# Attention over positions: block keys and values fetched by SyncE, queries read in place, score products of 64 x 64

## The reference

```python
x = x + attn(cond(x, cond_1024))         # causal attention inside each sequence, one head
h = cond2(x, cond_1024)                  # x + x @ layer, a matrix of its own for each sequence
# "ffn" on h, with S = 32 sequences as the attended axis and 256 positions as the batch:
ln1 = layer_norm(h); qkv = ln1 @ qkv_weight.T          # 16 query heads, 4 key/value heads, head size 16
scores = q . k * 16 ** -0.5, causal over the 32 sequences; attn = softmax(scores)
h1 = h + (attn @ v) @ proj_weight.T
# mixture of 8 experts, two per token: router, gelu(x @ w1) @ w2, weighted sum
x = x + h1 + moe(layer_norm(h1))
```

## Time and profile before

| | |
|---|---|
| time, median of 3 runs | 1201.92 us (1200.04 to 1207.69) |
| span of the profiled execution | 1207.2 us |
| time of the profiled execution | 1207.69 us (the only one of the three that is not shorter than the span) |
| opening | 0 to 399 us |
| positions' loop (mask products L1333) | 399.2 to 711.0 us |
| experts, overlapping the loop's end | from about 720 us to the end |
| busy over the span | PE 1128.8 (94%), PEld 1016.7 (84%), DVE 910.1 (75%), ACT 824.1 (68%), POOL 587.6 (49%) |
| mean granted TensorE clock | 0.968 of full speed |

### The profile page before, as it was taken

How to read it: one execution, slowest core, us unless ns; L and a number is a source line. 1 busy time by engine, 2 the same in 40 slices (tenths; PEclk the granted TensorE clock), 3 DMA queues, 4 the chain that set the end, 5 groups by cost and what they waited for, 6 DMA issues and landing times. The chain is left out here.

```text
span 1207.2 us, 25130 instructions
## 1 busy us (share of the span) xinstructions
PE 1128.8 (94%) x8180; PEld 1016.7 (84%) x8180; DVE 910.1 (75%) x2230; ACT 824.1 (68%) x1869; POOL 587.6 (49%) x564
## 2 busy tenths in 40 slices
PE   7899999999999899998998998899999999999994
PEld 4699999999998688877787776789998899889884
DVE  5677777677775579888898886897877777777872
ACT  2466666766666588887886778557677766776671
POOL 0012212122222144787888786678865454555446
PEclk9899999999999899998999998989999999999998
DMA  9533435343331022344444355578887686777654
GB/s 300 125 106 122 121 114 161 109 140 118 99 104 54 18 80 80 116 133 134 129 133 135 111 170 180 161 174 218 196 198 180 167 194 179 188 182 175 166 141 63
DMA packets 117838, 171.25 MB, mean 142 GB/s; under 512 B 13584, under 2 KB 88752, under 8 KB 117680
## 3 DMA queue, kind: packets, MB, share of 16 engines
q1 hardware_dynamic: 91120, 135.43, 36.7%
q0 software_dynamic: 26592, 34.24, 14.9%
HBM read 103.76 MB, written 67.69 MB: 142 GB/s over the span
## 5 line engine op out<-in xcount | busy, mean ns | idle before, releaser
L1311 POOL DMA_INDIRECT out_rows<-y,row x142 | 235.4, 1658 | 173.1 <-DVE y L1931 129.6
L1862 DVE TENSOR_TENSOR hl<-h,hh 128x512 fp32r<-128x512 f32 (+1 forms) x156 | 99.7, 642 | 83.7 <-ACT h L1530 73.0
L178 PE MATMUL gh<-w2h,hh 128*128 128x256 f32 x568 | 159.7, 281 | 1.1 <-issue 1.1
L180 PE MATMUL gh<-w2h,hl 128*128 128x256 f32 x568 | 159.8, 281 | 0.0
L179 PE MATMUL gh<-w2l,hh 128*128 128x256 f32 x568 | 159.6, 281 | 0.0
L1529 ACT ACTIVATE hh<-gw 128x512 fp32r<-128x512 f32 (+1 forms) x78 | 44.1, 565 | 126.9 <-issue 125.2
L1289 POOL DMA_INDIRECT slot_rows<-kept,slot x104 | 112.0, 1077 | 29.6 <-issue 28.4
L178 PEld LDWEIGHTS gh<-w2h,hh 128*128 128x128 f32 x568 | 107.8, 190 | 2.3 <-issue 1.2
L844 POOL TENSOR_SCALAR spread<-mv 128x2 f32<-128x2 f32 x32 | 7.0, 218 | 210.1 <-DVE mv L992 209.8
L179 PEld LDWEIGHTS gh<-w2l,hh 128*128 128x128 f32 x568 | 107.9, 190 | 1.1
L180 PEld LDWEIGHTS gh<-w2h,hl 128*128 128x128 f32 x568 | 107.8, 190 | 0.0
(11 more groups left out here) (338 smaller groups left out, 3945.9 us busy)
## 6 DMA issues: line engine op xcount, KB each, us to landing
w1e<-in_moe_w SPq DMA_DIRECT2D x39, 512.0 KB
w2e<-in_moe_w SPq DMA_DIRECT2D x39, 512.0 KB
xr<-slot_rows SPq DMA_DIRECT2D x32, 532.0 KB
x_rows<-x SPq DMA_DIRECT2D x64, 256.0 KB, 2.5
xg<-x_rows SPq DMA_DIRECT2D x62, 256.0 KB
xT<-in_xT SPq DMA_DIRECT2D x32, 256.0 KB, 2.8
x<-in_x SPq DMA_DIRECT2D x32, 256.0 KB, 3.7
out_rows<-res SPq DMA_DIRECT2D x64, 128.0 KB
```

What stands on the lines that cost most here:

```text
L178: nc.tensor.matmul(out, at_a(ah), at_b(bh), start=first, stop=False, skip_group_check=True)
L180: return nc.tensor.matmul(out, at_a(al), at_b(bh), start=False, stop=last, skip_group_check=True)
L1311: g.indirect_dma_start(out=out, out_offset=bass.IndirectOffsetOnAxis(ap=row[m % NR][:, t:t + 1], axis=0), in_=y[m % 2][:, t, :], in_offset ...
L1862: v.tensor_tensor(hl[m % 2][:, f, 0:n], h[:, f, 0:n], hh[m % 2][:, f, 0:n].bitcast(F32), ALU.subtract).then_inc(hl_did, 1)
```

## The change

Keys and values are no longer spread by VectorE. Three SBUF tensors, `keys0`, `keys1` and `values`, each for both places, are zeroed by GpSimd once; for every step SyncE copies the keys of each head into its block of columns, twice (once for each partition half), by 8 transfers, and the values by 8 more, from SBUF to SBUF. Keys have two buffers, values one. The queries are read where they are (`pr.heads`), with positions ahead of the channel half in their layout, so ScalarE's copies and VectorE's multiplication are gone. The scores of a place and position are two products of 64 rows x 64 columns x 128, one per partition half; TensorE does one half of both places, the transposes of place 0's values, the other half of both places, and the transposes of place 1's. The value product's output goes to both partition halves of `ps_w` in two products of 64 moving columns, and ScalarE takes it with one copy of 128 partitions. In the opening, `xT` and `stack` now share memory with `keys0` and `values`, and SyncE issues step 0's transfers at its end. SyncE's hardware loop is written out, each load stands ahead of its store, and the transfers of steps 1 and 2 go ahead of the loop, those of step j + 3 at the start of its step j.

```diff
@@ Program
+        self.keys0 = sb("keys0", [P, U2, NKV, TG, S])
+        self.values = sb("values", [P, U2, TG, NKV, S])
...
+    def fetch_keys(self, sp, keys, k):
+        groups = slice(U2 * k, U2 * (k + 1))
+        for side in range(2):
+            for g in range(NKV):
+                sp.dma_start(keys[side * NKV * HD + g * HD:side * NKV * HD + (g + 1) * HD, :, g].rearrange("p u t s -> p u (t s)"),
+                             self.kv[g * HD:(g + 1) * HD, groups].rearrange("p g t s -> p g (t s)")
+                             ).then_inc(self.keys_in[k % 2], 16)
+
+    def fetch_values(self, sp, k):
+        for g in range(NKV):
+            rows = slice((NKV + g) * HD, (NKV + g + 1) * HD)
+            for u in range(U2):
+                sp.dma_start(self.values[rows, u, :, g], self.kv[rows, U2 * k + u]).then_inc(self.values_in, 16)
@@ opening, SyncE
             pipeline(step, 0, I1 + 2)
+            sp.wait_ge(pr.cleared, 2)
+            for u in places:
+                after(sp, dve_did["kv"], I1 - 1, u)
+            pr.fetch_keys(sp, pr.keys0, 0)
+            pr.fetch_values(sp, 0)
@@ opening, GpSimd
-            pipeline(step, -2, I1 + 2)
+            pipeline(step, -2, I1 + 1)
+            for u in places:
+                after(pool, dve_did["u"], I1 - 1, u)
+            g.memset(pr.keys0[:], 0.0).then_inc(pr.cleared, 1)
+            for u in places:
+                after(pool, pe_did["layer"], I1 - 1, u)
+            g.memset(pr.values[:], 0.0).then_inc(pr.cleared, 1)
+            pipeline(step, I1 + 1, I1 + 2)
@@ rows_and_experts, SyncE
+            def blocks(k):
+                if k == 1:
+                    sp.wait_ge(pr.cleared, 3)
+                else:
+                    after(sp, pe_did["score"], k - 2, U2 - 1)
+                pr.fetch_keys(sp, keys[k % 2], k)
+                after(sp, pe_did["vT"], k - 1, U2 - 1)
+                pr.fetch_values(sp, k)
+
             def step(j):
+                if j + 3 < I2:
+                    blocks(j + 3)
+                if j == EARLY_STORES:
+                    sp.wait_ge(pr.planned, 1)
+                    sp.wait_ge(pr.scattered[0], 16 * K * EARLY_GROUPS)
                 for u in places:
                     after(sp, pool_did["res"], j, u)
                     if j + 1 < LAST:
                         load(j + 1, u)
                     store(j, u)
+            for u in places:
+                load(0, u)
+            for k in (1, 2):
+                blocks(k)
+            for j in range(EARLY_STORES):
+                step(j)
@@ TensorE
+            def score(k, u, side, t):
+                rows = slice(side * KV1, (side + 1) * KV1)
+                return t_.matmul(ps_s[u][rows, t * P:(t + 1) * P], pr.heads[rows, group(k, u), t, :],
+                                 keys[k % 2][rows, u, :, t, :], start=False, stop=True, skip_group_check=True)
...
                         t_.matmul(ps_s[u][:], pr.identb[:], pr.causalb[:].rearrange("p t g s -> p (t g s)"),
                                   start=True, stop=False, skip_group_check=True)
-                        after(pe, act_did["q"], k, u)
-                        after(pe, dve_did["kv"], k, u)
-                        for t in range(TG):
-                            ins = t_.matmul(ps_s[u][:, t * P:(t + 1) * P], qg[u][:, t].rearrange("p j s -> p (j s)"),
...
-                        ins.then_inc(pe_did["score"], 1)
+                    pe.wait_ge(pr.keys_in[k % 2], 16 * 2 * NKV * (k // 2 + 1))
+                    for t in range(TG):
+                        for u in places:
+                            score(k, u, u, t)
+                    pe.wait_ge(pr.values_in, 16 * U2 * NKV * (k + 1))
+                    values(k, 0)
+                    for t in range(TG):
+                        for u in places:
+                            ins = score(k, u, 1 - u, t)
+                            if t == TG - 1:
+                                ins.then_inc(pe_did["score"], 1)
+                    values(k, 1)
...
-                            ins = t_.matmul(ps_w[u][0:KV1, t * P:(t + 1) * P], vb[(k - 1) % 2][u][:, t, :],
-                                            pwT[u][:, t].rearrange("p j s -> p (j s)"), start=True, stop=True)
+                            for side in range(2):
+                                rows = slice(side * KV1, (side + 1) * KV1)
+                                ins = t_.matmul(ps_w[u][rows, t * KV1:(t + 1) * KV1], vb[(k - 1) % 2][u][:, t, :],
+                                                pwT[u][:, t, 2 * side:2 * side + 2].rearrange("p j s -> p (j s)"),
+                                                start=True, stop=True)
@@ ScalarE
-                if has(k + 1):
-                    heads(k + 1, 0)
...
-                        for jp in range(2):
-                            ins = a.copy(aoT[u][jp * KV1:(jp + 1) * KV1], pairs[:, jp])
-                        ins.then_inc(act_did["ao"], 1)
+                        a.copy(aoT[u][:], ps_w[u][:, 0:TG * KV1].rearrange("p (t h s) -> p h t s", t=TG, h=2)
+                               ).then_inc(act_did["ao"], 1)
@@ VectorE
-                if has(k + 1):
-                    for u in places:
-                        heads(k + 1, u)
-                        next(route, None)
@@ program
-            pr.q = kept[:, :, 0:DC * P].rearrange("p g (c t s) -> p c g t s", c=DC, t=TG)
+            pr.q = kept[:, :, 0:DC * P].rearrange("p g (t c s) -> p c g t s", c=DC, t=TG)
+            pr.heads = kept[:, :, 0:DC * P].rearrange("p g (t n) -> p g t n", t=TG)
```

More of the change, by code:

```diff
@@ L382, in __init__ @@
         self.blank = sb("blank", [P, ROW])
+        self.keys_in = [self.sem(f"keys_in{n}") for n in range(2)]
+        self.values_in, self.cleared = self.sem("values_in"), self.sem("cleared")
         self.scattered = [self.sem(f"scattered{k}") for k in range(3)]
@@ L431, in opening @@
         x = bufs("x", [P, TC, D])
-        xT = bufs("xT", [P, DC, T])
-        stack = bufs("stack", [STACK, 2, D])
+        xT = [pr.keys0[:, u].rearrange("p g t s -> p (g t s)").rearrange("p (c n) -> p c n", c=DC) for u in places]
+        stack = [pr.values[0:STACK, u].rearrange("p t g s -> p (t g s)").rearrange("p (k n) -> p k n", k=2) for u in places]
         uT = parts("uT", [P, DC, T])
@@ L1054, in rows_and_experts @@
         KV1 = NKV * HD
-        qg = brief("qg", [KV1, TG, JQ, S])
-        kvd = brief("kvd", [P, TG, NKV, S])
-        last12 = [a[:].rearrange("p t g s -> p (t g s)").rearrange("p (k n) -> p k n", k=2) for a in kvd]
+        keys1 = passing.enter_context(nc.sbuf_tensor("keys1", [P, U2, NKV, TG, S], F32))
+        keys = [pr.keys0, keys1]
+        last12 = [pr.keys0[:, u].rearrange("p g t s -> p (g t s)").rearrange("p (k n) -> p k n", k=2) for u in range(U2)]
         rows12 = lambda j, u: last12[u] if j == LAST else x12[u][:]
@@ L1255, in _ @@
             g = nc.gpsimd
+            g.memset(keys1[:], 0.0).then_inc(pr.cleared, 1)
             g.memset(half[:], -0.5).then_inc(halved, 1)
@@ L1559, in take_ranks @@
                 a.copy(ranks[:, 0:n], ps_h[0][:, D + P:D + P + n]).then_inc(rank_out, 1)
-            def heads(k, u):
-                if k > 0:
-                    after(act, pe_did["score"], k - 1, u)
-                a.copy(qg[u][0:KV1].rearrange("p t j s -> p j t s")[:, 0::2], pr.q[0:KV1, :, group(k, u)])
-                a.copy(qg[u][0:KV1].rearrange("p t j s -> p j t s")[:, 1::2],
-                       pr.q[KV1:P, :, group(k, u)]).then_inc(act_did["q"], 1)
             def step(k, has):
@@ L1767, in place @@
                     dve.sem_inc(pr.planned, 1)
-            def heads(k, u):
-                if k > 0:
-                    after(dve, pe_did["score"], k - 1, u)
-                    after(dve, pe_did["vT"], k - 1, u)
-                v.tensor_tensor(kvd[u][:], pr.kv[:, group(k, u)].unsqueeze(2).broadcast_to([P, TG, NKV, S]),
-                                pr.cst[:, C_HEAD:C_HEAD + NKV].unsqueeze(1).unsqueeze(3)
-                                .broadcast_to([P, TG, NKV, S]), ALU.mult).then_inc(dve_did["kv"], 1)
             def step(k, has):
```

45 lines of the change are left out of this document (14 added, 31 removed).

## The result

The changed kernel takes 1314.33 us (median of 4 runs, 1308.26 to 1322.28) against 1204.81 for the kernel before beside it: a ratio of 1.0913, 95% interval 1.087 to 1.0956. Slower, as forecast, but by 110 us instead of 21. The profiled execution is the one of 1308.26 us. Medians here are taken over the executions in the faster of the chip's two states; that leaves out one of the four of the kernel with only the keys by transfers (1249.72 us).

What follows compares the result with a forecast made beforehand. The order inside a step was taken as the bound, with TensorE's work and the score-to-logits chain equally long. Loop +16, start +6, ScalarE -1 made +21 on 1201.9: 1223 us, range over the cases 1203 to 1253.

Steps and rivals of the forecast that it cites:

- the term "Transfers": SyncE in each loop step: 20 issues at 0.46 us make 9.2 us, under a step of 10.3.
- The forecast's own sign of being wrong: Loop: the forecast is wrong if TensorE waits for the transfers in each step.
- Rival 3: SyncE is the bound: from 0.55 us an issue, 20 make 11.0 us a step; 1243 us, chance 12%.
- Rival 5: A transfer so late that a step waits for it each time; 1270 us, chance 3%.
- First maximum at 3.1 instead of 1.50: Plain step: with the new score order VectorE starts its first maximum 3.1 us into the step instead of 1.50.
- rival 1: Small score products don't overlap and stay 0.11 us apart; +42 us, 1265 us, chance 8%.
- Value product 0.26 longer: TensorE in each step: 32 records take 2.15 to 2.2 us, 0.26 more than the 16 before.
- Rival 2: Value product's column halves serialize at 0.11 us a record, 1.6 us a step; near 1268 us, chance 5%.
- A plain step of 10.26: Loop step with VectorE's plain stretch of 2.82: 10.26 us, against 8.95 before.
- the 13 short steps: Loop steps of 8.9 to 9.4 us: 10.5 us against a mean of 9.08, +18.4 us in all.
- Start of the loop: Before step 3: first transfers delay the second stage to near 403.2, step 1's values add about 3; +6 us (3 to 12).
- The tail at zero: Behind step 31: the tail has no score, so its time changes by zero.

Runs made afterwards that it cites:

- the square: Changed kernel, its score order kept or each place's records together: 1314.33 and 1315.86 us with transfers, 1226.42 and 1218.20 without those of steps 4 to 31.
- the better version: Kernel before with value product in column halves, one aoT copy, SyncE's loop written out and load ahead of store: 1200.49 us, ratio 0.9957.

## Why the forecast was wrong

**The step that failed is the term "Transfers": 20 issues a step at 0.46 us, 9.2 us together, hidden under a step of 10.3.** The price came from the earlier trace rows, and those are transfers from HBM with one run a partition. The new ones stay within SBUF, and 0.59 us for one, 0.64 from start to start, is their price even alone on the chip. In the loop they average 0.63 (24 of the 557 issues take 0.9 to 1.8), and loads and stores rose too, xg's from 0.38 to 0.53. One step's sum: 16 x 0.67 + 2 x 0.57 + 2 x 0.50 = 12.9 us, against the measured 12.99. The forecast's own sign of being wrong came with it: TensorE waits for the values in 25 of the 28 steps. Rival 3 named this mechanism, with its threshold at 0.55 an issue and a price of 1243; its chance (12%) and above all its price were too low, because it stopped at the threshold instead of asking what each further 0.1 us costs: 20 x 0.1 x 28 = 56 us. Rival 5 had the mechanism at a higher price, 1270, still 44 short. The 0.83 of the earlier trace rows, which the forecast put beside rival 3, is no support for it: it is two issues, 0.42 each.

**Covers compared too closely.** 9.2 of work under a cover of 10.3 leaves 0.055 us an issue. Nothing in the trace priced a transfer within SBUF, so a fair upper end of that term lay far above the range's 1253.

**First maximum at 3.1 instead of 1.50: right in kind and size.** It is 3.23 in the changed kernel's free step and 3.05 in the run without transfers; the value product, forecast at 7.2, begins at 7.16 in the first. Score records 0.055 apart (forecast 0.06), in overlapping pairs: rival 1 is refuted.

**Value product 0.26 longer: wrong sign.** It is 0.6 to 0.8 us shorter, 1.17 to 1.28 us for 32 records. The two column halves on the same 128 rows run side by side: the two records of a pair start 0.007 us apart and the next pair 0.058 us later, where one record of twice the columns took 0.11. The forecast had carried over 0.06 from row halves. The Trainium skill (TensorE: Matmul & The Clock Gate, Packing small matmuls) lets a weight load overlap a matmul in flight only where the row group differs; these records share all rows, and here 32 loads and 32 matmuls take 1.17 us together, so the measurement goes against that sentence. Rival 2 is refuted.

**A plain step of 10.26: it is 9.40** without the transfers. The first maximum comes 0.05 earlier than forecast, VectorE's stretch is 0.09 shorter, the piece behind it 0.07, the value product 0.87; only the logits are 0.22 longer than the 0.92 that the forecast had taken over unchanged. So without its transfers the changed loop is 2 us longer than the old one, not 16: the 13 short steps cost 10 us (forecast 18), the 13 middle ones gain 1 (forecast a loss of 1), and the two long ones gain 7 (forecast 5).

**Start of the loop: right within what the starts vary.** The second stage begins at 403.5 (forecast 403.2), step 3 6.1 us later (forecast 6). But in the unchanged starts step 3 lies anywhere between 426.2 and 431.7, in the changed ones between 432.5 and 439.1, and with keys alone at 422.7 and 423.3.

**The tail at zero: wrong by 12 us**, and not explained (above).

Added up by the medians: some 88 us for SyncE's issuing (1314.33 to 1226.42), 8.2 for the late report (to 1218.20), 12.4 for the rest over 1205.8, of which the profile of that run shows 8: 9 in the experts' stage and 5 at the start, less 6 in the loop. The other 4 are that the two profiled executions lie off their medians. That the medians come from different series is part of the uncertainty; their runs don't overlap in either of the first two steps.

That SyncE sets the pace is shown from both sides, by taking the transfers away and by adding them unread. That the late report costs 8 us, and nothing while SyncE is full, is shown by the square. That the transfers crowd the loads out on the DMA engines, rather than in SyncE's queue, is the rival that no run takes away by itself; against it speak SyncE's missing idle time, the DMA engines' share of busy time (0.39 in the changed loop and with sixteen unread transfers, 0.41 before), and that twelve unread transfers cost only a fifth of what sixteen do. That the clock gives back part of the better version's gain is read from its windows alone and was not tried.

## What to carry to other kernels

A queue that only issues has a budget like any engine: count all its issues in a step, price each by the nearest row with the same two memories and the same pattern, and where there is no such row, work out what a dearer issue would cost, since beyond the step the full excess is paid in every step. Here a sum at 90% of the step by the wrong rows (9.2 of 10.3) was the bound by the right ones. Sixteen small transfers at 0.64 us of issue apiece are no bargain for two VectorE products of 0.68 us. Removing work from engines that only fill gaps (VectorE and ScalarE lost 89 us of work in this loop) need not buy anything: with the transfers gone and the order mended the changed loop takes 276.6 us (at a clock of 0.94), and the kernel before with its written-out SyncE loop 276.0 (at 0.99). The one part that shortened TensorE's own chain, column halves on disjoint columns, was the part worth keeping.

## What the runs showed of the hardware that was not expected

- An issue on SyncE takes 0.42 to 0.45 us between HBM and SBUF with one run a partition, and 0.59 to 0.62 within SBUF, whether it moves 8 KB or 128 KB. The Trainium skill (DMA: Bandwidth & Descriptors, Issuing engines are not separate DMA queues) calls the time to initiate a transfer usually small relative to the transfer: for one it is a third here (0.6 beside a landing of 1.8 us); summed over twenty in a 10 us step it is more than the step.
- Two fp32 products on disjoint column halves of the array, same rows, overlap: 32 records of 64 moving columns in 1.17 us, a pair every 0.058 us.
- GpSimd's plain issue of the same transfer, 0.51 us, is shorter than SyncE's.
- The granted clock fell to 0.83 in steps that followed one with TensorE 99% busy (8.44 us, then 9.98 for the same work). It fell as well where TensorE waits most (0.89 in the changed kernel's loop, 0.82 with sixteen unread transfers), so a busy TensorE is not the only thing before such a fall.
